# Narrow attention scores on four row groups of TensorE, context products moved between PSUM banks, and constant products at both ends

## What is computed

```python
# narrow (0 and 3)
xn = rmsnorm(x, norm_w)
q = (xn @ wq).reshape(B, T, 16, 8); k, v = cond @ wk, cond @ wv    # 4 heads of 8
attn = softmax(einsum('btgrd,bsgd->bgrts', qg, k) / sqrt(8))
x = x + einsum('bgrts,bsgd->btgrd', attn, v) @ wo
# wide (1 and 2)
q, k, v = x @ Wq, ctx @ Wk, ctx @ Wv                               # 16 heads of 64
probs = softmax(einsum('bhqd,bhkd->bhqk', q, k) / 8 + col_bias)
x = einsum('bhqk,bhkd->bhqd', probs, v) @ Wo + bo + x
```

## Time and profile before

| | |
|---|---|
| median of three runs | 381.04 us |
| the profiled execution | 380.89 us |
| its span, first to last instruction | 379.1 us |
| outside the span | 1.8 us |
| TensorE busy | 359.7 us (95%) |
| VectorE / ScalarE / GpSimd busy | 267.7 / 279.0 / 187.6 us |
| mean granted TensorE clock | 0.986 of 2.4 GHz |

### The profile page before, as it was taken

One profiled execution on the slowest core, in us unless ns is written; L12 is line 12 of the kernel. 1 busy time (PEld: TensorE's weight loads), 2 busy tenths in 40 slices (PEclk: granted clock), 3 DMA queues, 4 the chain that ended last, 5 costly groups with the idle time before them and its releaser, 6 DMA issues.

```text
span 379.1 us, 10494 instructions
## 1 busy us (share of the span) xinstructions
PE 359.7 (95%) x3522; PEld 319.1 (84%) x3522; DVE 267.7 (71%) x1401; ACT 279.0 (74%) x1176; POOL 187.6 (49%) x220
## 2 busy tenths in 40 slices
PE   8889999999999999999999999999999999978665
PEld 8787799899999998889889988888999989867554
DVE  2999975636536547696978886577564785699982
ACT  4889998865665567475899999998566865647793
POOL 3677853733223236454676765443333435447662
PEclk9899999999999999999999999999999999999979
DMA  7925000000000000000000000000000000000000
GB/s 232 411 66 216 1 3 3 2 3 2 1 2 3 2 0 3 2 3 0 10 3 9 9 8 2 3 3 2 0 3 2 3 2 1 2 3 3 7 9 14
DMA packets 4883, 9.91 MB, mean 26 GB/s; under 512 B 608, under 2 KB 3296, under 8 KB 4576
## 3 DMA queue, kind: packets, MB, share of 16 engines
q1 hardware_dynamic: 4400, 8.91, 6.5%
q10 hardware_dynamic: 432, 0.34, 0.4%
HBM read 8.73 MB, written 0.52 MB: 24 GB/s over the span
## 4 chain that ended last, share of the span: by engine, by line
PE 74%; DVE 21%; ACT 3%; issue 1%; DVEq 0%; POOL 0%; POOLq 0%
PE pt_ps L849 13%; PE scores_ps L836 9%; DVE probs L615 8%; PE q_ps L796 8%; PE fill_ps L701 7%; PE v_ps L900 7%; PE v_ps L882 7%; PE fill_ps L702 7%; PE fill_ps L703 7%; PE v_ps L870 3%; DVE probsT L626 3%; ACT probs L482 3%; PE q_ps L788 2%; DVE qn L598 2%; DVE qn L594 2%; PE scores_ps L825 2%
## 5 line engine op out<-in xcount | busy, mean ns | idle before, releaser
L482 ACT ACTIVATE probs<-probs,negmax 128x128 f32<-128x128 f32 x512 | 198.5, 391 | 81.0 <-DVE negmax L615 80.9
L379 POOL TENSOR_TENSOR probs<-probs,inv 128x512 f32<-128x512 f32 x128 | 137.3, 1075 | 176.8 <-DVE inv L622 176.4
L482 ACT ACTIVATION_READ_ACCUMULATOR probs<-probs,negmax 128x1 f32 x512 | 96.8, 189 | 0.0
L615 DVE CUSTOM_DVE_ANT_0 probs<-scores_ps,col_bias 128x128 f32<-128x128 f32 x256 | 58.2, 284 | 39.1 <-PE scores_ps L836 39.1
L849 PE MATMUL pt_ps<-smalls,probs 128*128 128x128 f32 x512 | 70.5, 282 | 6.2 <-DVE probsT L626 6.2
L849 PEld LDWEIGHTS pt_ps<-smalls,probs 128*128 128x128 f32 x512 | 57.6, 143 | 18.2 <-issue 14.8
L615 DVE CUSTOM_DVE_ANT_0 probs<-scores_ps,no_bias,inv_rms 128x128 f32<-128x128 f32 x224 | 64.2, 343 | 5.8 <-PE scores_ps L825 5.4
L626 DVE COPY probsT<-pt_ps 128x512 f32<-128x512 f32 x96 | 63.0, 684 | 2.6 <-PE pt_ps L849 0.5
L615 DVE DVE_READ_ACCUMULATOR2_ANT negmax<- 128x1 f32 x512 | 42.5, 83 | 0.0
L701 PE MATMUL fill_ps<-c_hi,w_hi 128*128 128x256 f32 x128 | 38.3, 300 | 0.0
L836 PE MATMUL scores_ps<-kT,qT 64*128 64x128 f32 x512 | 37.2, 285 | 0.0
(11 more groups left out here) (92 smaller groups left out, 583.2 us busy)
## 6 DMA issues: line engine op xcount, KB each, us to landing
kT<-in_kv_w SPq DMA_DIRECT2D x6, 512.0 KB, 6.4
w_qo<-in_qo_w SPq DMA_DIRECT2D x2, 1024.0 KB, 8.3
v<-in_ctxT SPq DMA_DIRECT2D x4, 256.0 KB, 9.5
v<-in_kv_w SPq DMA_DIRECT2D x2, 512.0 KB, 11.2
outT<-x SPq DMA_DIRECT2D x8, 64.0 KB, 1.6
wn<-in_narrow_w SPq DMA_DIRECT2D x2, 192.0 KB, 5.7
x<-in_xT SPq DMA_DIRECT2D x1, 384.0 KB, 8.1
oT<-in_narrow_kv ACTq DMA_DIRECT2D x1, 256.0 KB, 3.9
```

Source lines behind the costliest of these rows:

```text
L379: nc.gpsimd.tensor_tensor(p4, p4, inv[:, o % 2, side, :].unsqueeze(2).broadcast_to([P, 4, S]), ALU.mult,).then_inc(probs_made[side], 1)
L482: last = nc.scalar.activation(e, e, ACT.Exp, scale=-1.0, bias=negmax[:, o % 2, side, q:q + 1], accum_out=rowsum[:, o % 2, side, q:q + 1])
L615: last = nc.vector.tensor_tensor_reduce(out=probs[:, o % PROBS_RING, side, cols], in0=banks[scores_bank(o)][side][:, cols], in1=bias, scal ...
```

## The change

- Narrow queries are one float32 product of 128 columns (`narrow_queries` of TensorE) into 128 columns of `v_ps`, beside the mean of squares, in the even half before the job. VectorE makes `qn` with one operation on 128 x 128, now at the start of the odd half, behind `mean_out` and ahead of `scores_out`.
- Narrow scores are four float32 products of 32 rows and 512 columns, one for each row group, each into its own bank (two score banks A0, A1 and two former fill banks B0, B1). All four are made at the start of the even half, for both octets of the job, once all four banks are free.
- The splitting of narrow keys on GpSimd, ScalarE and VectorE is left out; `kn` and `kd` are float32 in 128 rows.
- Context products have a bank named in `FILLS`. In narrow stages they use A0 and A1 in even halves (two each) and the queries' bank Q0 in odd halves (one each); in wide stages they use B0 and B1. "k1.1" and "k1.2" move from half 7 to half 8 (and "k1.3" from 8 to 9), "v6.0" from half 39 to half 40, "k4.0" from 25 to 24, "k6.0" stays in 37.
- The weights of narrow queries shrink from 384 to 128 columns a layer, those of narrow keys grow from 96 to 128 columns a chunk.
- Constant products (`warm_up`): three more in half 0, and four into `q_ps` in each half from 58 to 65, ahead of the transposes.

```diff
-NQ, NO = 0, 2 * REP * STACK
+
+
+NQ, NO = 0, 2 * C
 NARROW_COLS = NO + 2 * C
-NK, NV = 0, 2 * CC * STACK
+NK, NV = 0, 2 * CC * P
...
+A0, A1, B0, B1, Q0 = range(5)
 FILLS = {
...
-    5: ["v0.2", "bias"], 6: ["v0.3", "k1.0"], 7: ["k1.1", "k1.2"],
-    8: ["k1.3"], 9: ["v1.0"], 10: ["v1.1", "kn0.3"], 11: ["v1.2", "vn2"], 12: ["v1.3", "k2.0"], 13: ["k2.1"],
...
-    24: ["v3.3"], 25: ["k4.0", "kn2.0"], 26: ["k4.1", "vn3"], 27: ["k4.2"], 28: ["k4.3"], 29: ["v4.0", "kn3.0"],
...
-    36: ["v5.2", "v5.3"], 37: ["k6.0"], 38: ["k6.1", "k6.2"], 39: ["k6.3", "v6.0"],
...
+    -1: [("kn0.0", Q0)],
+    0: [("vn0", Q0), ("kn1.0", A0)], 1: [("k0.0", Q0)], 2: [("k0.1", A0), ("k0.2", A1)], 3: [("k0.3", Q0)],
+    4: [("vn1", A0), ("v0.0", A1)], 5: [("v0.1", Q0)], 6: [("bias", A0), ("v0.2", A1)], 7: [("v0.3", B0), ("k1.0", B1)],
+    8: [("k1.1", B0), ("k1.2", B1)], 9: [("k1.3", B0), ("v1.0", B1)], 10: [("kn0.3", B0), ("v1.1", B1)],
...
+    24: [("v3.3", A0), ("k4.0", A1)], 25: [("kn2.0", Q0)], 26: [("k4.1", A0), ("k4.2", A1)], 27: [("vn3", Q0)],
+    28: [("k4.3", A0), ("v4.0", A1)], 29: [("kn3.0", Q0)], 30: [("v4.1", A0), ("v4.2", A1)], 31: [("v4.3", Q0)],
...
+    40: [("v6.0", B1)], 41: [("v6.1", B0)], 43: [("kn2.3", B1), ("v6.2", B0)], 44: [("v6.3", B1)], 45: [("k7.0", B0)],
...
+def scores_bank(o, side):
+
+    return 2 * (o % 2) + side if is_narrow(o // 2) else side
+
+
+def bank_uses():
+
+    order = [[] for _ in range(5)]
+    for o in range(-1, 2 * NJOBS):
+        n, h = o // 2, o % 2
+        octets = [o, o + 1] if is_narrow(n) and h == 0 else [] if is_narrow(n) or o < 0 else [o]
+        for octet in octets:
+            for side in range(2):
+                order[scores_bank(octet, side)].append((octet, side))
+        for name, bank in FILLS.get(o, []):
+            order[bank].append(name)
+        if o >= 0 and is_wide(n + 1):
+            order[Q0].append(("queries", n + 1, h))
+    return order
+
+
+BANK_USES = bank_uses()
+
+FIRST_WAIT = 58
...
-            def split_keys(name):
-
-                i = KN_ORDER.index(name)
-                pool.wait_ge(fill_read[fill_bank(name)], fill_count(name))
-                nc.gpsimd.tensor_copy(kn[0:STACK, i % 2], kn_raw[0:STACK, i % 2]).then_inc(kn_rounded, 1)
-                pool.wait_ge(kn_rounded, i + 1)
-                low = slice(2 * PART, STACK)
-                nc.gpsimd.tensor_tensor(kn[low, i % 2], kn_raw[low, i % 2], kn[low, i % 2].bitcast(F32), ALU.subtract
-                                        ).then_inc(kn_split, 1)
-
             def diagonal_keys(n):
 
                 l, b = job(n)
-                i, order = narrow_index(n), KN_ORDER.index(f"kn{b // 2}.{l}")
-                pool.wait_ge(kn_split, order + 1)
+                i, name = narrow_index(n), f"kn{b // 2}.{l}"
+                pool.wait_ge(bank_read[FILL_BANK[name]], count_of(FILL_BANK[name], name))
                 if i >= KD_RING:
-                    pool.wait_ge(scores_full[1], 2 * NARROW_JOBS[i - KD_RING] + 2)
...
+                    pool.wait_ge(bank_full[B1], count_of(B1, (2 * NARROW_JOBS[i - KD_RING] + 1, 1)))
+                keys = kn[:, KN_ORDER.index(name) % 2, b % 2 * S:(b % 2 + 1) * S]
+                shape = [P, KV_HEADS, S]
+                nc.gpsimd.tensor_tensor(kd[:, i % KD_RING], keys.unsqueeze(1).broadcast_to(shape),
+                                        rep_mask.unsqueeze(2).broadcast_to(shape), ALU.mult).then_inc(kd_made, 1)
...
-            def first_keys_rest():
-
-                dve.wait_ge(kn_rounded, 1)
-                low = slice(2 * PART, STACK)
-                nc.vector.tensor_tensor(kn[low, 0], fill_ps[fill_bank("kn0.0")][low, 0:PAIR], kn[low, 0].bitcast(F32),
-                                        ALU.subtract).then_inc(kn_split, 1)
-                dve.wait_ge(kn_split, 1)
-                dve.sem_inc(fill_read[fill_bank("kn0.0")], 1)
-
             def mean_out(n):
 
                 dve.wait_ge(ms_full, narrow_index(n) + 1)
+                dve.wait_ge(qn_full, narrow_index(n) + 1)
                 nc.vector.tensor_scalar(rms[:, n % 2:n % 2 + 1], ms_ps[:, 0:1], EPS, None, ALU.add
                                         ).then_inc(rms_out, 1)
 
             def narrow_queries(n):
 
-                use = narrow_index(n) + 1
-                dve.wait_ge(q_full, uses(n, 0))
-                all_parts = qn[0:STACK, n % 2].rearrange("p r t -> p (r t)")
-                nc.vector.tensor_scalar(all_parts, q_ps[0:STACK, :], -NARROW_SCALE, None, ALU.mult).then_inc(qn_hi_made, 1)
-                dve.wait_ge(qn_hi_made, use)
-                low = slice(PART, 2 * PART)
-                rest = qn[low, n % 2].rearrange("p r t -> p (r t)")
-                nc.vector.scalar_tensor_tensor(
-                    out=rest, in0=q_ps[low, :], scalar=-NARROW_SCALE, in1=rest.bitcast(F32),
-                    op0=ALU.mult, op1=ALU.subtract).then_inc(qn_lo_made, 1)
-                dve.wait_ge(qn_lo_made, use)
-                dve.sem_inc(q_read, 1)
+                dve.wait_ge(qn_full, narrow_index(n) + 1)
+                nc.vector.tensor_scalar(qn[:, n % 2], qn_ps, -NARROW_SCALE, None, ALU.mult).then_inc(qn_made, 1)
...
                 if h == 1 and is_narrow(n + 1):
                     mean_out(n + 1)
+                    narrow_queries(n + 1)
...
-                for m in NARROW_JOBS:
-                    if m > 0 and query_half(m) == o - 1:
-                        narrow_queries(m)
...
-                    for r in range(REP):
-                        first = NQ + (NARROW.index(l) * REP + r) * STACK
-                        last = nc.tensor.matmul(q_ps[0:STACK, r * T:(r + 1) * T], wn[:, first:first + STACK], x[:, b, :],
-                                                start=True, stop=True)
-                    last.then_inc(q_full, 1)
-                    return
...
+            def narrow_queries(n):
+
+                l, b = job(n)
                 if n >= 3:
                     pe.wait_ge(v_read, uses(n - 3, 1))
-                if n > 0 and is_narrow(n - 1):
-                    pe.wait_ge(rms_out, narrow_index(n - 1) + 1)
+                if n > 0:
+                    pe.wait_ge(rms_out, narrow_index(n))
+                    pe.wait_ge(qn_made, narrow_index(n))
+                pe.wait_ge(sq_ready, narrow_index(n) + 1)
                 nc.tensor.matmul(ms_ps, x_sq[:, n % 2, :], mean_w[:, 0:2], start=True, stop=True).then_inc(ms_full, 1)
-
-            def scores(n, h):
+                if l == 0:
+                    pe.wait_ge(x_loaded[0 if b < 2 else 1], 16)
+                else:
+                    pe.wait_ge(y_read, JOBS.index((2, b)) + 1)
+                    pe.wait_ge(norms_folded, 2)
+                first = NQ + NARROW.index(l) * C
+                nc.tensor.matmul(qn_ps, wn[:, first:first + C], x[:, b, :], start=True, stop=True).then_inc(qn_full, 1)
...
+            def narrow_scores(n):
+
+                i = narrow_index(n)
+                for r in range(REP):
+                    free_bank(r, (2 * n + r // 2, r % 2))
+                pe.wait_ge(kd_made, i + 1)
+                pe.wait_ge(qn_made, i + 1)
+                for r in range(REP):
+                    rows = slice(PART * r, PART * (r + 1))
+                    nc.tensor.matmul(banks[r][:], qn[rows, n % 2, :], kd[rows, i % KD_RING].rearrange("p g k -> p (g k)"),
+                                     start=True, stop=True).then_inc(bank_full[r], 1)
...
-                if l in NARROW:
-                    i = narrow_index(n)
-                    pe.wait_ge(kd_made, i + 1)
-                    pe.wait_ge(qn_lo_made, i + 1)
-                    keys = kd[0:STACK, i % KD_RING].rearrange("p g k -> p (g k)")
-                    for side in range(2):
-                        nc.tensor.matmul(out[side][:], qn[0:STACK, n % 2, 2 * h + side, :], keys, start=True, stop=True
-                                         ).then_inc(scores_full[side], 1)
-                    return
...
+                    pe.wait_ge(qn_made, narrow_index((o + 4) // 2) + 1)
...
-                if valid(o):
-                    scores(n, h)
+                if is_wide(n):
+                    wide_scores(n, h)
+                if is_narrow(n) and h == 0:
+                    narrow_scores(n)
+                if o == 0:
+                    warm_up(3)
+                if o >= FIRST_WAIT and valid(o - 2):
+                    pe.wait_ge(bank_read[Q0], len(BANK_USES[Q0]))
+                    warm_up(4, q_ps)
                 if valid(o - 3) and is_wide((o - 3) // 2):
                     weighted_values((o - 3) // 2, (o - 3) % 2)
                 if valid(o - 2):
                     transpose_probs(o - 2)
                 if valid(o - 3) and is_narrow((o - 3) // 2):
                     weighted_values((o - 3) // 2, (o - 3) % 2)
-                for name in FILLS.get(o, []):
+                for name, bank in FILLS.get(o, []):
                     project_context(name)
-                for m in NARROW_JOBS:
```

(11 more changed lines are left out.)

162 lines of the change are left out of this document (71 added, 91 removed), and 7 rows, old and new, of the table FILLS.

## The result

The changed kernel takes 386.14 us (median of four runs, 386.10 to 387.81), beside 380.97 us for the kernel before on the same chip (four runs). The ratio is 1.0136, 95% interval 1.0102 to 1.0170: **1.4% slower**, where 375.6 us was forecast and 384 was the upper end. The profiled execution has a span of 383.8 us. Three single executions further down are left out of medians and ranges, because they ran at little over half the granted clock (581.74 us of e1_between, 577.65 of e13_outs2) or stood apart from the others of their kernel (392.65 of e2_noconst).

A forecast was written before the change was run, and what follows sets the result against it. TensorE was taken to bound B, D and nearly all of C, VectorE and its waits A and E. From 380.9 us, -5.0 + 1.55 + 1.7 + 0.85 - 4.5 = -5.4 gave 375.5, forecast as 375.6; range 370.5 to 384.

The forecast's parts named there:

- C: Stage of narrow jobs 12 to 19, 81.1 us before; forecast to grow by 1.7 us.
- the release of TensorE by VectorE: Last term of a narrow job's loop: last accumulator and semaphore before the next scores, taken as about 0.2 us.
- E: Last stage, narrow jobs 28 to 31 and the end, 51.7 us before; forecast to shrink by 4.5 us.
- constant products counted as hidden: Last stage: 0.85 us per half, mostly hidden where TensorE waited 1.03 for a transposes' bank; about 0.4 not in half 65.
- A: First stage, narrow jobs 0 to 3, 8.3 to 53.7 us; forecast -5.0 us, with longer than 41 us a wrong sign.
- the scores: Narrow scores on TensorE: four row groups working side by side, 1.06 us per job against 2 x 0.55 before.
- B: First stage of wide jobs, 105.9 us before, TensorE always busy; forecast to grow by 1.55 us.
- D: Second stage of wide jobs, 86.7 us before, TensorE always busy; forecast to grow by 0.85 us.
- the loop: Narrow job: scores, output projection, add_input, reading of the odd octet, next scores; 9.7 us against 8.8 of TensorE's own work.
- The clock's worth: Last two jobs: constant products keep the granted clock from falling, worth about 1.5 us.
- rival (4): The tail gains nothing, as constant products and four banks held together take back VectorE's saving; 379.5 us, chance 0.10.
- the row groups: Narrow scores rivals: partial overlap, 379 us, chance 0.12; overlap only in pairs or product by product, 386.5 to 392, chance 0.16.

The follow-up runs named there:

- e1_between: The changed kernel with the next job's queries and the output projection between the two context products of even narrow halves; 378.50 us, ratio 0.9921.
- e13_outs2: The kernel of e11_outs once more on the same chip, with no further edit; 374.35 us, ratio 0.9823.
- e2_noconst: The changed kernel without the constant products of halves 58 to 65; 389.48 us, ratio 1.0192.
- e3_constwait: The changed kernel with four constant products ahead of a context product in odd halves 29, 31, 33, 35 and 37; 388.28 us, ratio 1.0182.
- e5_consts: e1_between with constant products of halves 58, 60, 62 moved to the ends of 57, 59, 61 and none in 65; 376.90 us, ratio 0.9886.
- e11_outs: e9_best with VectorE copying the wide outputs between the two sides of the scores in halves 56 and 58; 374.60 us, ratio 0.9841.
- e9_best: e1_between plus half 7's context products moved to half 8, constant products at ends of 59 and 61, none in 57, 58, 60, 62; 376.46 us.
- e10_copies: e9_best with VectorE instead of ScalarE copying the second side of the transposes of octets 3, 4 and 5; 376.43 us, ratio 0.9873.

## Why the prediction was wrong

**The steps that failed.** In C, the term for the release of TensorE by VectorE (0.2, measured 0.44), in a loop that was otherwise right. In E, a wait that the sum left out, for VectorE's copy out of `v_ps`, and constant products counted as hidden that stand on the chain. In A, ScalarE's idle time, taken as time that can all go.

**Right: the scores, B, D and the loop's existence.** 1.06 forecast, 1.07 measured; B +1.55 and D +0.85, measured +1.55 and +0.75. The extrapolation from column groups of 32 and row groups of 64 held. Eight records at 0.43, the spacing of the earlier trace rows, are 3.4 us and took 1.07 here, a speedup of 3.2. The Trainium skill (TensorE: Matmul & The Clock Gate, Measured speedup vs the span model) gives a speedup of 3.07 for four row groups of 32 rows and 512 columns. The trace is a little above the page's figure, and both are far from no overlap.

**C: the mechanism was right, its terms too small.** The loop was forecast at 9.7 and is 10.02. Term by term: scores 1.07 (1.06 forecast); from the transposes to the projection 5.38, 194.37 to 199.75 (5.23 with the query product, which takes 0.30 and not 0.21); projection to add_input 0.43 (0.51); add_input and `mean_out` 0.27 (0.27); queries 0.20 (0.20); two sides 2.23 (2.23); from the start of the last accumulator read to TensorE's start **0.44 (0.2)**. The failed step is that last one, 0.24 of the 0.32: I had no row for a release of TensorE by VectorE's reading and took half of what it is. With it jobs 14 to 17 change by about +0.6 each where +0.3 was forecast, job 18 by +1.28 (+0.95), job 13 by +0.75 (+0.4), job 12 by +0.09 (-0.3); job 19's -0.57 was right (-0.55). Sum +4.0. That the loop binds is shown: e3_constwait adds 4.3 us of work to TensorE for nothing, and the order of e1_between, read in the trace of e5_consts, takes it away. A deeper fault is that I took the loop as given and priced it, though 2.9 us of context products that no one in the loop needs stood in my own sum.

**E: an omitted wait and a mispriced cover.** Half 55 gave -1.39 (-1.5 forecast). Job 28 came to 9.99 (8.45), job 29 to 10.17 (9.2), job 30 to 8.64 (7.75), and the rest to the last add_input to 15.96 (15.0). I summed VectorE's work in these jobs as if TensorE's part of the loop started when TensorE was ready. In jobs 28 and 29 it starts when VectorE has copied the wide outputs out of `v_ps`, behind both sides of the even octet: TensorE is idle for 1.06 us in job 28, and in job 29 the copy stands in the chain behind its constant products. e11_outs, which moves that copy ahead in two halves, takes 2.0 out of E. And I wrote that the constant products are hidden in the wait for a transposes' bank; behind the new order part of them is on the chain (1.09 us at 358.03), and another placing of them, in e9_best, gives 0.8 back. The clock's worth was about right: 1.5 forecast, 1.9 by the one trace of e2_noconst. E as a whole came out as rival (4) had it, with no gain (-0.08), at a chance of 0.10. Mending these two steps, in e9_best and e11_outs, gave back 2.8 of the 4.4; how the rest divides is not shown.

**A: the limit that I named and then let go.** I wrote that ScalarE, busy 40.9 of 45.4, "lets some 4.5 go", as if all its idle time could vanish, and took off 1.0 for copies that move away. ScalarE in A after, in three stretches (the fourth busy column; it is also full from 20 to 30):

```profile
30.00:33.00 3.00, 1.28 (x28) 1.01 (x16) 2.96 (x21) 1.65 (x6) 0.69 (x1) 1.00 0.27 115
33.00:42.00 9.00, 8.09 (x81) 6.26 (x80) 8.05 (x44) 8.87 (x36) 8.02 (x8) 1.00 0.01 2
42.00:52.21 10.21, 8.54 (x60) 7.03 (x52) 8.13 (x34) 10.05 (x39) 5.93 (x6) 1.00 0.01 3
```

From 20 us on ScalarE is all but full except for 1.35 us at 30 to 33; before 20 it is idle for 1.1. In that gap it waits for VectorE's reading of scores, and so does TensorE, for 1.72 us ahead of a context product. The chain of the kernel after shows what VectorE does meanwhile; L539 to L546 are `match_tokens`, the set-up of the column bias, which it makes in one go from 27.68 to 31.05:

```profile
27.99 0.98 DVE tok_f L540
...
30.38 0.67 DVE qT L546 x3
...
32.19 0.30 PE scores_ps L677
```

The same block stands in the chain of the kernel before (30.20 to 33.65), and no run here moves it: that is a rival repair left untested. ScalarE's busy time in A did not fall either (41.17; 40.90 before). The 1.0 that I took off for copies came as 0.5: the stage has eight copies of wide context products instead of nine, and 64 exponentials instead of 62, 1.4 us more with their accumulator reads. A could lose what was idle (4.5 us before, 2.7 after) and lost 1.5 in all; at 43.91 it is also longer than the 41 that I had named as a sign of being wrong. Taking A and B together is surer, since products can be moved between them: 151.33 before, 151.35 after, 151.82 in e9_best, 151.73 in e10_copies, 151.13 in e11_outs. **No version gained more than 0.2 there**: the 3.8 us less that VectorE is busy in A (41.90 to 38.09; 4.8 forecast) bought nothing measurable. e10_copies shows that ScalarE limits A too.

**The sum.** C's error (+2.3), E's (+4.4) and A's (+3.5, and up to 1.6 more where the clock falls) make the 10 us. I gave the slower side 19%, nearly all of it to the row groups, and priced those rivals for 13 jobs, without a reason why not for all 16 narrow ones. The mechanism that did decide, the loop, was in my forecast itself, but with a release of 0.2 and no wait for `v_ps`. The 0.2 us for the larger loads came to nothing that can be seen in the stages: the transfer of narrow key and value weights landed after 4.2 us instead of 3.9.

**The repair.** With the projection ahead of the second context product, fewer context products in A, the constant products behind what VectorE waits for, and the outputs copied between the sides, the kernel takes 374.60 and 374.35 us in two sets of runs, 1.6 to 1.8% less than before and 3% less than the changed kernel. Of the 11.6 us between the changed kernel's trace (383.8) and that of e11_outs (372.2), 8.6 are C's and come from the one moved step.

## What to carry to other kernels

When a change makes two engines wait for each other once per job, write the loop down with every term and ask of each whether the next engine needs it: what it doesn't need goes behind what it does. An engine's idle time is no room until the trace says what it waits for. And look at the chain for long blocks that are not in the loop, such as the set-up of the bias here. Constant products belong behind the work that another engine waits for, and each place has to be tried: in this kernel they were worth 1.9 us at the end (in one trace) and nothing at the start, where the kernel with them took 1.7 us more.
